# Thirty-two key units dealt out anew over a four-chunk recurrence, six of them behind it

## The reference, cut to what matters

```python
# x [16, 64, 256], ctx [16, 64, 128]; 16 heads
x = layernorm(x + attn(x))        # a chunked recurrence, then @ Wo
x = layernorm(x + xattn(x, ctx))  # cross attention, 16 heads of 128
x = layernorm(x + ffn(x))         # quantised feed-forward
def attn(x):                      # T = 64 in 4 chunks of 16, heads of 16
    for each chunk c:
        kh = k[c] @ S                          # state products
        v_new = gradient_of_layernorm_loss(kh) # a long row-wise chain
        A = tril(q[c] @ k[c].T) * eta
        qh = q[c] @ S - A @ v_new              # own terms
        o[c] = q[c] + layernorm(qh)
        S = S - (k[c] * eta).T @ v_new
    og = o * sigmoid(x @ Wg1 @ Wg2)
    return rmsnorm_per_head(og) * norm_w @ Wo
def xattn(h, ctx):
    q = rmsnorm(h @ Wq, gq); k = rmsnorm(ctx @ Wk, gk)   # per head of 128
    return softmax(q @ k.T / sqrt(128)) @ (ctx @ Wv) @ Wo
```

## Time and profile before

| | us |
|---|---|
| median of 3 runs (400.85, 404.96, 407.01) | 404.96 |
| the profiled execution, its own time | 404.95 |
| its span, from the first to the last instruction | 403.4 |

### The profile page before, as it was taken

One profiled execution on the slowest core, in us unless ns is written; L12 is line 12 of the kernel. 1 busy time (PEld: TensorE's weight loads), 2 busy tenths in 40 slices (PEclk: granted clock), 3 DMA queues, 4 the chain that ended last, 5 costly groups with the idle time before them and its releaser, 6 DMA issues.

```text
span 403.4 us, 11509 instructions
## 1 busy us (share of the span) xinstructions
PE 343.7 (85%) x5050; PEld 241.7 (60%) x5050; DVE 259.8 (64%) x508; ACT 190.6 (47%) x354; POOL 107.4 (27%) x117
## 2 busy tenths in 40 slices
PE   3899979978788765499899999999999999988932
PEld 3343865534444322298688796887968879663711
DVE  0588938199899997615435574856748567394564
ACT  3043984553635343034725555555555655554110
POOL 3025495800000000000043251523515334062001
PEclk9999997999989889569999999999999999997865
DMA  8992000000500200157010010101102000000000
GB/s 253 252 351 99 1 2 6 5 3 5 159 5 19 93 2 11 56 112 158 2 55 0 26 30 15 52 2 33 36 13 54 2 15 0 16 0 13 2 1 26
DMA packets 17633, 19.99 MB, mean 50 GB/s; under 512 B 3360, under 2 KB 15024, under 8 KB 17328
## 3 DMA queue, kind: packets, MB, share of 16 engines
q1 hardware_dynamic: 17552, 19.24, 17.5%
q10 hardware_dynamic: 32, 0.02, 0.0%
HBM read 18.07 MB, written 1.18 MB: 48 GB/s over the span
## 4 chain that ended last, share of the span: by engine, by line
PE 64%; DVE 20%; ACT 7%; issue 4%; POOL 2%; DMA 1%; SPq 1%; POOLq 0%; ACTq 0%; DVEq 0%
PE ps L636 15%; PE ps L702 12%; PE ps L454 5%; PE ps L694 5%; PE ps L542 4%; PE ps L679 4%; PE ps L721 3%; PE ps L652 2%; PE ps L561 2%; PE ps L745 2%; PE ps L579 2%; DMA wg<-in_L_attn_Wg_dram 1%; PE ps L739 1%; PE ps L670 1%; PE ps L661 1%
## 5 line engine op out<-in xcount | busy, mean ns | idle before, releaser
L636 PEld LDWEIGHTS ps<-x1t,xwq 128*128 128x128 f32 x512 | 62.1, 199 | 7.7 <-issue 4.9
L636 PE MATMUL ps<-x1t,xwq 128*128 128x128 f32 x512 | 65.0, 286 | 1.5 <-ACT x1t L1026 1.5
L702 PE MATMUL ps<-mvo,cxp 128*128 128x256 f32 x256 | 59.1, 386 | 0.1
L1542 POOL TENSOR_SCALAR rstd<-mv 128x1 f32<-128x1 f32 x22 | 4.8, 218 | 187.3 <-DVE mv L1361 187.3
L702 PEld LDWEIGHTS ps<-mvo,cxp 128*128 128x128 f32 x256 | 48.2, 193 | 6.8 <-issue 0.7
L542 PE MATMUL ps<-ctxt,xwk 128*128 128x512 f32 x64 | 39.3, 728 | 0.0
L990 ACT ACTIVATE qt<-ps 128x512 f32<-128x512 f32 x32 | 19.1, 597 | 37.5 <-PE ps L636 37.5
L916 ACT ACTIVATE ksq<-ps 128x512 f32<-128x512 f32 x32 | 19.0, 593 | 31.9 <-PE ps L542 23.0
L1414 DVE TENSOR_TENSOR gs<-ps,s 128x352 f32<-128x352 f32 x16 | 8.4, 525 | 20.9 <-PE ps L721 20.9
L918 ACT ACTIVATE kt<-ps,gks 128x512 f32<-128x512 f32 x32 | 21.9, 683 | 0.0
L694 PE MATMUL ps<-pt,ctx 64*128 64x512 f32 x64 | 21.0, 665 | 1.0 <-ACT pt L1016 0.7
(11 more groups left out here) (215 smaller groups left out, 667.6 us busy)
## 6 DMA issues: line engine op xcount, KB each, us to landing
rkb<-kscale SPq DMA_DIRECT2D x16, 256.0 KB, 4.0
xn<-in_x_dram SPq DMA_DIRECT2D x4, 512.0 KB, 5.4
ctx<-in_ctx_dram SPq DMA_DIRECT2D x4, 512.0 KB, 7.9
xwo<-in_L_xattn_Wo_dram SPq DMA_DIRECT2D x1, 2048.0 KB, 14.2
xwq<-in_L_xattn_Wq_dram SPq DMA_DIRECT2D x4, 512.0 KB, 4.1
w1n<-in_L_ffn_w_gate_up_dram SPq DMA_DIRECT2D x1, 1408.0 KB, 8.9
xwv<-in_L_xattn_Wv_dram SPq DMA_DIRECT2D x1, 1024.0 KB, 11.0
xwk<-in_L_xattn_Wk_dram SPq DMA_DIRECT2D x1, 1024.0 KB, 16.5
```

The costliest lines, as they stand in the source:

```text
L636: last = mm(bank(n % 2, P, t * P), xwq[qn][:, k * BANK + t * P:k * BANK + (t + 1) * P], x1t[:, (i % 2) * D + k * P:(i % 2) * D + (k + 1) * ...
L702: last = mm(bank(6 + turn_of[("y", i, 0)] % 2, D), cxp[:, h * P:(h + 1) * P], mvo[:, h * D:(h + 1) * D], start=h == 0, stop=h == XH - 1)
```

## The change

The lists of chunks 0 and 1 are cut to 4 and 6 units, and six units go behind the last own terms: on PE in one row, on ACT three before `output_root(7)` and three before `output_root(8)`, with the 33rd call behind that root. Chunks 2 and 3 keep their counts and places, but their units are numbers 10 to 25 and no longer 16 to 31, so the key sums fall at other places in them.

```diff
-KEY_PLACES = [(2, 1, 2, 2, 1), (1, 2, 1, 1, 2, 1), (1, 2, 1, 1, 2, 1), (1, 2, 3, 2)]
+KEY_PLACES = [(1, 1, 1, 1, 0), (1, 1, 1, 1, 1, 1), (1, 2, 1, 1, 2, 1), (1, 2, 3, 2)]
+KEYS_LAST = 6
...
                 own_terms(c, 1)
                 for n in places:
                     keys(n)
+            keys(KEYS_LAST)
             key_unit(next(units))
...
                 gated_square(c - 1)
                 keys(places[-1])
             output_root(2 * NCH - 2)
+            keys(KEYS_LAST // 2)
+            output_root(2 * NCH - 1)
+            keys(KEYS_LAST // 2)
+            output_root(2 * NCH)
             key_unit(next(units))
-            output_root(2 * NCH - 1)
-            output_root(2 * NCH)
```

## The result

Four runs of the changed kernel gave 407.98, 410.00, 416.10 and 416.11 us, median 413.05; four of the kernel before beside them had a median of 404.02. Two of the four runs of the change, the profiled one among them, are slower executions at a lower granted clock, and every ratio here leaves such runs out. The ratio is 1.0167 with a 95% interval of 1.0093 to 1.0241: slower, by 6.7 us on 404.02 where 2.35 were predicted. The interval excludes no change and also excludes the predicted 1.0058 (407.3 on 404.95); whether the loss is above 2% it leaves open.

A forecast was written before the change was run, and what follows sets the result against it. It took PE's wait for 256-instruction code blocks as the bound in chunks 0 and 1. Loads +2.5, chunks 2 and 3 +0.3, tail +1.05 and clock -1.5 gave +2.35 on 404.95: 407.3 us, range 400.5 to 411.0.

The forecast's parts named there:

- Code blocks bound chunks 0 and 1: In chunks 0 and 1 PE waits for its 256-instruction code blocks, each step at least 3.45 to 4.1 us.
- Their gain, -3.55 by the boundary in `own_terms(1, 1)`: Six fewer units in chunks 0 and 1 bring the boundary from 102.05 to 98.5: 3.55 us won.
- The other bound, 1.5 with 3.8 a step: In chunks 0 and 1, the gain is only 1.5 us if every code step took 3.8 us.
- Then the loads: At `state_products(2, 0)`, PE's code comes 0.15 to 0.45 us behind bulk loads and waits them out; chunk 2 begins 2.5 later.
- Chunks 2 and 3, +0.3: Sums at other places bring `own_terms(2, 1)` close to its need in chunk 2, +0.3 us (0 to 1.4); chunk 3 unchanged.
- caught one chunk later: Code for `state_products(3, 0)` is held by the second loads instead; chunk 2 grows by 5.4 us, total 406.7; chance 0.12.
- The tail, +1.05: ACT's output roots stand behind units in the tail: +0.4, +0.55 and +0.1 us for roots 6, 7, 8; range 0.6 to 2.0.
- The clock, -1.5 (0 to -4): Units fill PE's idle gap before `ttt_out`, so it and later query quarters run at higher clock: -1.5 us.
- What was hidden, stayed hidden: In the tail, later `krow`, SP's round trip and the fourth `xwq` quarter stay hidden; 0.5 us reaches DVE if late.

The follow-up runs named there:

- empty_head: The changed kernel with no key units in chunks 0 and 1 and 16 behind the last own terms; 414.06 us in a single execution.
- head_only: The kernel before, with the change's ten units in chunks 0 and 1 but the six removed put into chunk 3; 410.76 us, ratio 1.0161.
- twelve_head: The changed kernel with two units moved back from the tail: twelve in chunks 0 and 1, four in the tail; 402.21 us, ratio 0.9963.
- spread_sums: The changed kernel with key sums done one by one, behind the next unit but one, not in groups of four; 413.07 us, ratio 1.0185.
- late_loads: The changed kernel with loads of the second and third `xwq` quarters waiting for the own terms of (3, 0); 410.39 us, ratio 1.0118.
- tail_only: The kernel before, chunks 0 to 2 unchanged, with six units moved from chunk 3 into the change's tail; 405.10 us, ratio 1.0017.
- before_root6: The kernel before with only ACT's order changed: root 6 ahead of the last two units, root 7 ahead of the 33rd call; 401.74 us, ratio 0.9961.
- after_again: The changed kernel with only an empty line added, for its second profile; 409.61 us in a single execution.
- head_late: The kernel before with ten units in chunks 0 and 1, six more in chunk 3, second and third `xwq` quarter loads delayed; 411.03 us, ratio 1.0112.

## Why the prediction was right in part, and where it was wrong

Slower by little and within 2% is what it said, and the change is slower by 1.67%. That is partly luck: the largest term of its sum stood for something that did not happen, and two terms close to nothing came out large. The size was 4.4 us short. Two of the four times (407.98 and 410.00) lie in its range of 400.5 to 411.0, two above it.

- *Code blocks bound chunks 0 and 1: right.* Boundaries, counts and standstills lie where they were predicted, and in empty_head a third less work of PE gains no time there. The Trainium skill (Runtime: NRT & Kernel Launch, section Instruction fetch mechanics) calls such a crossing "mostly hidden"; this case's standstills of 0.35 to 3.75 us disagree.
- *Their gain, -3.55 by the boundary in `own_terms(1, 1)`: mis-sized.* From the first scores on it was 1.64 (44.32 us against 45.96). Nine steps took 32.8 us and not 31.6, 3.64 each, and the boundary in `own_terms(0, 0)` ahead of them came 0.7 later than counted. Choosing 3.45 for all steps with over 100 small loads behind was the error, and empty_head's 3.6 to 4.0 show the same. The other bound, 1.5 with 3.8 a step, was nearer by chance: nine steps of 3.8 would leave 0.95.
- *"Then the loads", +2.5 at chunk 2: wrong.* This is the step that failed. It rested on a packet that starts 1.5 to 1.8 us behind its boundary when a key follows within 7 small loads, and on code 0.15 to 0.45 behind the first load being held to the end of the loads. Neither holds. With the same 7 loads behind it the packet started 1.0 behind its boundary in the first profile (102.02 to 103.0), ahead of the loads by 0.3, and 1.6 behind in the second, where the loads were 0.24 ahead and PE still went on 2.4 us behind the packet. Chunk 2 began 0.2 earlier than before, 1.8 measured from the first scores (0.55 in the second profile). What sets 1.0 or 1.6 stays open.
- *Chunks 2 and 3, +0.3: mis-sized, and the main error.* It measured +5.8 (+4.3 in the second profile). I had seen that groups of sums now stand before `scores_ttt(3, 0)` and `own_terms(2, 1)`, and priced their instructions, but neither their waits for ACT's squares nor that the next block of code comes late behind such a wait. head_only has the same loss without the new tail, and twelve_head, with the sums at their old places, has neither late packets of that kind nor the loss. Late code is at most 2.1 us of it (3.2 in the second profile), by PE's standstills at the two boundaries. spread_sums has packets on time and is as long, so how the rest divides between the wait and the sums themselves was not shown. late_loads says what the catch by the loads adds: 2.4 us (0.9 against the second profile), behind 3.4 of PE's lateness.
- *The rival "caught one chunk later": happened in effect.* Its condition, a slip of the boundary in `own_terms(2, 1)` from +21.1 to +23.2, was passed with +24.7. That its price of 5.4 is close to the 5.8 is luck: it was to be the catch alone, which measured 0.9 to 2.4.
- *The tail, +1.05: mis-sized.* +4.8 and +3.8, and +2.2 in tail_only, where PE is not late. I gave root 6 0.4 us for a group of sums; its unit and sums ran at half clock and late, and it came 3.1 late (0.1 in tail_only). Root 7 behind three units was to cost 0.55 and cost 1.6 to 2.0: ACT waits 1.19 us for PE's group of sums among those units, in both kernels.
- *The clock, -1.5 (0 to -4): not tested cleanly.* The last stage was +0.7 in the first profile, -4.6 in the second, -3.9 in tail_only. PE's idle time before `ttt_out` was 2.30 us, near the predicted 2.5, but `ttt_out` took 3.66 and 3.49 us in the change, against 1.99 in tail_only behind the same 2.30. And before_root6, with the gap unfilled and 3.78 for `ttt_out`, was 4.3 shorter than the kernel before. The 8.50 for a query quarter, from which the term was worked out, is thus what one execution showed, not the cost that the kernel before always pays.
- *What was hidden, stayed hidden.* The reciprocal of the key roots stood at 182.6 beside work of PE from 182.23 on, and the fourth quarter of `xwq` was issued at 179.8.
- *Not predicted at all:* 1.6 us in a preparation that the change does not touch. The sixteen matmuls of its first projection take 7.1 us in the kernel before and five of the experiments, whose first scores lie at 56.0 to 56.1, and 8.7 to 10.1 us in the change and the other seven, with first scores at 57.7 to 59.2. It goes with the program, since the second profile of the change repeats it (57.7, 57.8). Why is left open.

## What to carry to other kernels

Where a timeline says "issue" every 256 instructions, count instructions, not engine time: removing work from such a stretch gains little or nothing (24.2 against 24.3 us with eight units gone), and a move of a few instructions shifts where the boundaries fall for the rest of the program. Then look for waits in the first instructions behind each boundary, and for bulk loads issued shortly before one: either can delay the next block. In a tail of one engine, put the short instruction that it waits for ahead of filler work in its supplier's program; that alone took 1.3 us off the stretch. And take more than one profile of each kernel: two executions of the changed one differ by 5.3 us in its last stage.

## What the runs showed of the hardware that was not expected

- Behind a wait of PE's for a semaphore the next block of PE's code comes late. A wait up to some 76 instructions behind a boundary delayed the packet: 111.12 to 115.0, 124.64 to 127.84, each 1.1 us behind the end of the square that it waited for; 3.2 us in after_again, 4.2 in head_only. Without such a wait packets start 1.0 to 1.8 us behind the boundary. How far into a block the request really stands was not measured.
- With a queue of loads ahead of it, of some 4 to 6 us, a code packet comes at their end (109.5 before, 134.34 after). A packet just behind the first of the loads (0.24 to 0.37 us in after_again, twelve_head and head_late), or 0.3 us ahead of them, is not held.
- A group of two 128x32 weight loads between 128x512 matmuls costs about 1.0 us (129.56 to 130.53), as much as a group of eight (1.0 in the prediction's rows). Of these two sizes the small one is dear by the group, not by the instruction.
- In empty_head PE had a third less work in a stretch, was granted 0.60 in place of 0.86 and finished it no sooner.
